# GpSimd kept to transfers in the block loop, and the pass over all tokens moved behind block 20

## The reference

```
s = attention(xn)          # 4 heads; per token and head a layernorm of 32 numbers, times gamma = 1 + ln_w
g = silu(moe(xn))          # each token goes to 1 of 8 experts:
                           #   y = (a * sigmoid(gate)) @ w2[e] + b2[e],  [a, gate] = xn @ w1[e] + b1[e]
out = x + s * g            # elementwise, per token
```

## Time and profile before

| | |
|---|---|
| median of 3 runs | 222.67 us (221.75 to 223.59) |
| the profiled execution's own time | 222.88 us |
| its span, first to last instruction | 221.0 us |
| TensorE busy | 197.2 us, 89% |
| VectorE busy | 162.3 us, 73% |
| ScalarE busy | 148.2 us, 67% |
| GpSimd busy | 127.6 us, 58% |
| mean granted TensorE clock | 0.972 of full speed |

### The profile page before, as it was taken

How to read it: one execution, slowest core, us unless ns; L and a number is a source line. 1 busy time by engine, 2 the same in 40 slices (tenths; PEclk the granted TensorE clock), 3 DMA queues, 4 the chain that set the end, 5 groups by cost and what they waited for, 6 DMA issues and landing times.

```text
span 221.0 us, 5891 instructions
## 1 busy us (share of the span) xinstructions
PE 197.2 (89%) x1790; PEld 164.7 (75%) x1790; DVE 162.3 (73%) x428; ACT 148.2 (67%) x318; POOL 127.6 (58%) x154
## 2 busy tenths in 40 slices
PE   7998998899999999999999999899999998998000
PEld 6887855355555555799999998799999997997000
DVE  5999588869688777558879989986444699987400
ACT  2388858899888798678877777467777776673000
POOL 5575960556577772003333448787677598477740
PEclk9999999999999999999999999999999999999855
DMA  5999999971499612210870667265432975511100
GB/s 165 304 391 415 390 203 208 209 186 40 147 331 353 219 62 88 82 36 27 243 246 18 187 183 207 87 189 152 121 113 74 293 269 164 158 34 47 48 0 0
DMA packets 35103, 36.96 MB, mean 167 GB/s; under 512 B 4219, under 2 KB 29828, under 8 KB 35073
## 3 DMA queue, kind: packets, MB, share of 16 engines
q1 hardware_dynamic: 29762, 26.71, 37.3%
q0 software_dynamic: 4144, 9.79, 17.9%
q10 hardware_dynamic: 1168, 0.10, 0.4%
HBM read 21.95 MB, written 15.63 MB: 170 GB/s over the span
## 4 chain that ended last, share of the span: by engine, by line
PE 54%; DVE 17%; POOL 12%; issue 7%; DMA 4%; DVEq 1%; ACT 1%; POOLq 1%; ACTq 0%
PE bank L1293 14%; PE head_bank L1293 14%; PE bank L1302 13%; POOL xs_sorted L494 9%; DVE stats L799 3%; PE bank L1263 2%; PE head_bank L1251 2%; POOL out_x L539 2%; PE head_bank L1221 2%; PE bank L1180 2%; DMA x_sb<-in_L_attn_x 1%; DVE dm L1065 1%; PE bank L1241 1%; PE head_bank L1149 1%; DVE ffn L1082 1%
## 5 line engine op out<-in xcount | busy, mean ns | idle before, releaser
L518 POOL DMA_INDIRECT y_tokens<-ffn,idx x24 | 25.6, 1067 | 40.7 <-DVE ffn L1082 34.8
L676 ACT ACTIVATE wc<-w_sb 128x1024 f32 (+1 forms) x39 | 37.8, 970 | 15.2 <-issue 15.2
L494 POOL DMA_INDIRECT xs_sorted<-xn,pos x32 | 31.4, 982 | 21.9 <-DVE pos L936 9.3
L1302 PE MATMUL bank<-w_sb,dm 128*128 x312 | 41.7, 277 | 2.5 <-DVE dm L1065 2.5
L1302 PEld LDWEIGHTS bank<-w_sb,dm 128*128 128x128 f32 x312 | 38.0, 192 | 3.4 <-issue 3.3
L1293 PE MATMUL bank<-xsT,wc 128*128 128x128 f32 x320 | 39.1, 275 | 0.0
L1293 PEld LDWEIGHTS bank<-xsT,wc 128*128 128x128 f32 x320 | 37.3, 192 | 0.2 <-issue 0.2
L964 DVE TENSOR_TENSOR cm<-dm,head_bank 128x1024 f32<-128x1024 f32 (+1 forms) x32 | 29.1, 950 | 11.1 <-PE head_bank L1251 10.0
L1293 PE MATMUL head_bank<-xsT,wc 128*128 128x128 f32 x304 | 37.0, 275 | 0.0
L1293 PEld LDWEIGHTS head_bank<-xsT,wc 128*128 128x128 f32 x304 | 35.5, 192 | 0.0
L654 ACT ACTIVATE dm<-bank 128x512 f32<-128x512 f32 x48 | 26.9, 596 | 3.8 <-PE bank L1241 3.5
(11 more groups left out here) (189 smaller groups left out, 351.1 us busy)
## 6 DMA issues: line engine op xcount, KB each, us to landing
x_sb<-in_L_attn_x SPq DMA_DIRECT2D x16, 256.0 KB, 4.8
w_sb<-in_L_ffn_w SPq DMA_DIRECT2D x8, 512.0 KB, 8.5
w_sb<-negated_rows POOLq DMA_DIRECT2D x8, 508.0 KB
xs_sb<-xs_sorted SPq DMA_DIRECT2D x13, 192.0 KB, 2.6
xs_sorted<-b_sb SPq DMA_DIRECT2D x1, 2048.0 KB, 10.8
y_tokens<-zeros SPq DMA_DIRECT2D x1, 2048.0 KB
s_and_x<-x_sb SPq DMA_DIRECT2D x16, 128.0 KB
s_and_x<-xn SPq DMA_DIRECT2D x16, 128.0 KB
```

Source lines behind the costliest of these rows:

```text
L494: pool.indirect_dma_start(xs_dram, bass.IndirectOffsetOnAxis(ap=pos[:, t:t + 1], axis=0), xn[:, t, :], None).then_inc(s_scat, 16)
L518: pool.indirect_dma_start(y_dram, bass.IndirectOffsetOnAxis(ap=idx[:, j:j + 1], axis=0), ys_sb[:, j // CH % 2, j % CH, :], None, bounds_ch ...
L676: act.activation(wc[:, j % 3, h0:H2], w1_sb[:, bass.ds(e, 1), h0:H2], ACT.Copy).then_inc(s_wc, 1)
L1302: last = pe.matmul(bank[6 + j % 2][:, 0:D], uT[:, j % 2, c, :], w2_sb[:, bass.ds(e * (HC * D) + c * D, D)], start=(c == 0), stop=(c == HC ...
```

## The change

The change does six things.

- The factor gamma leaves GpSimd. It becomes 8 more steps of the normalisation on VectorE (4 tiles each), so there are 43 steps. STEPS_AT gives two steps to each of the iterations 12 to 19, where before it did so for 12 to 15.
- All 8 sums with x are on VectorE; GpSimd had 5 of them.
- LATE is 18 where it was 15, so 21 blocks (0 to 20) are scattered to `y_tokens`, and 18 take the late way.
- The pass is placed earlier: its products in iterations 25 to 28 (before 28 to 31), its sums in 27 to 31 (before on GpSimd and in 32), the joins two by two from iteration 32 to 40.
- SyncE stores all quarters of s behind the load of the rows of blocks 27 to 29 (c = 9), each when its two steps of gamma are done. Gathers 0 and 1 stand behind scatters 18 and 19, all others behind scatter 20.
- GpSimd has a `drain` in four places: before the first scatter, before scatters 6 and 12, and before the wait for `s_out`. The drains show in no row of the orders below.

The gathered rows and the late blocks' rows find place in `u_all`, in `right` (no longer used then) and in what is left of `cm`.

```diff
-    NSTEPS = 35
-    SMALL = 27
+    NSTEPS = 43
+    SMALL = 35
-    STEPS_AT = {2: 1, 3: 1, 4: 2, 5: 1, 6: 2, 7: 1, 8: 5, 9: 5, 10: 5, 11: 4, 12: 2, 13: 2, 14: 2, 15: 2}
-    GAMMA_AT = {11: 0, 12: 1, 14: 2, 15: 3}
-    LATE = 15
+    STEPS_AT = {2: 1, 3: 1, 4: 2, 5: 1, 6: 2, 7: 1, 8: 5, 9: 5, 10: 5, 11: 4}
+    STEPS_AT.update({j: 2 for j in range(12, 20)})
+    LATE = 18
-    PRODUCTS_AT = {28: (0, 1), 29: (2, 3), 30: (4, 5), 31: (6, 7)}
-    ADDS_AT = {32: (5, 6, 7)}
-    POOL_ADDS = (0, 1, 2, 3, 4)
-    JOINS_AT = {33: (0, 1), 34: (2, 3), 35: (4, 5), 36: (6, 7), 37: (8, 9), 38: (10,), 39: (11, 12), 40: (13, 14)}
+    PRODUCTS_AT = {25: (0,), 26: (1, 2), 27: (3, 4), 28: (5, 6, 7)}
+    ADDS_AT = {27: (0,), 29: (1, 2, 3), 30: (4, 5, 6), 31: (7,)}
+    JOINS_AT = {32 + i: (2 * i, 2 * i + 1) for i in range(9)}
-    TOKENS_AT.update({17: (6, 7), 18: (8,), 20: (9,), 22: (10,), 25: (11,), 28: (12,)})
-    GATHERS_AT = {18: (0,), 19: (1,), 20: (2,), 21: (3,), 22: (4,), 23: (5, 6, 7)}
-    ROWS_AT = {8: (0,), 9: (1, 2, 3)}
+    TOKENS_AT.update({17: (6, 7), 18: (8,), 20: (9,), 23: (10,), 26: (11,), 28: (12,)})
+    GATHERS_AT = {18: (0,), 19: (1,)}
+    ROWS_AT = {9: (0, 1, 2, 3)}
...
             def s_rows(g):
-                sp.wait_ge(s_gm, g + 1)
+                sp.wait_ge(s_norm, SMALL + 2 * (g + 1))
...
             for g in range(NPC):
-                if g in POOL_ADDS:
-                    sp.wait_ge(s_finp, POOL_ADDS.index(g) + 1)
-                else:
-                    sp.wait_ge(s_finv, g + 1 - len([i for i in POOL_ADDS if i < g]))
+                sp.wait_ge(s_finv, g + 1)
...
+            pool.drain()
             pool.wait_ge(s_yz, 16)
             for j in range(JL):
+                if j in (6, 12):
+                    pool.drain()
                 pool.wait_ge(s_ye, j + 1)
...
-                if j in GAMMA_AT:
-                    scaled(GAMMA_AT[j])
...
-            gather(8)
-            add_x(0)
-            add_x(1)
-            gather(9)
-            add_x(2)
-            add_x(3)
-            gather(10)
-            add_x(4)
-            for i in range(11, LATE):
+            for i in range(2, LATE):
                 gather(i)
+            pool.drain()
             pool.wait_ge(s_out, 16 * NPC)
...
+                dve.wait_ge(s_gamma, 2)
+                for ts in pieces:
+                    yield dve.tensor_tensor(sq[:, ts, :, :], sq[:, ts, :, :],
+                                            gamma[:, :].rearrange("p (h d) -> p h d", h=NH).unsqueeze(1).to_broadcast([P, 4, NH, DH]),
+                                            ALU.mult)
```

More of the change, by code:

```diff
@@ L109, in mlstm_moe_block @@
         u_flat = u_all[:, :, :, :].rearrange("p t h c -> p (t h c)")
-        gx = u_flat[:, 0:LATE * 2 * D].rearrange("p (i c) -> p i c", c=2 * D)
+        n_u = T * NH * DA // (2 * D)
         wc = sb("wc", [P, 3, H2])
@@ L195, in mlstm_moe_block @@
         ssum, den, rden, coef, nveps, na, nb_, ny, ny2 = [cflat[:, n * T * NH:(n + 1) * T * NH] for n in range(9)]
-        lz = cflat[:, 9 * T * NH:9 * T * NH + LATE * D].rearrange("p (i d) -> p i d", d=D)
+        c_free = 9 * T * NH
+        r_flat = right[:, :, :, :].rearrange("p h j s -> p (h j s)").bitcast(F32)
+        gx = [u_flat[:, i * 2 * D:(i + 1) * 2 * D] if i < n_u else cflat[:, c_free + (i - n_u) * 2 * D:c_free + (i - n_u + 1) * 2 * D]
+              for i in range(LATE)]
+        c_free += (LATE - n_u) * 2 * D
+        n_r = NH * NBS * S // 2 // D
+        lz = [r_flat[:, i * D:(i + 1) * D] if i < n_r else cflat[:, c_free + (i - n_r) * D:c_free + (i - n_r + 1) * D]
+              for i in range(LATE)]
         ys_sb = ffn[:, 0:2 * CH * D].rearrange("p (i n d) -> p i n d", i=2, n=CH)
@@ L323, in mlstm_moe_block @@
         s_yz = sem("s_yz")
-        s_gm = sem("s_gm")
         s_sx = sem("s_sx")
@@ L328, in mlstm_moe_block @@
         s_finv = sem("s_finv")
-        s_finp = sem("s_finp")
         s_fin = sem("s_fin")
@@ L498, in gather @@
                 pool.wait_ge(s_idx, (JL + i) // CH + 1)
-                pool.indirect_dma_start(gx[:, i, :], None, sx_dram, bass.IndirectOffsetOnAxis(ap=idx[:, JL + i:JL + i + 1], axis=0),
+                pool.indirect_dma_start(gx[i], None, sx_dram, bass.IndirectOffsetOnAxis(ap=idx[:, JL + i:JL + i + 1], axis=0),
                     bounds_check=NTOK - 1, oob_is_err=False).then_inc(s_gx[i], 16)
[L502 to L512, removed]
+            pool.drain()
             pool.wait_ge(s_yz, 16)
             for j in range(JL):
+                if j in (6, 12):
+                    pool.drain()
                 pool.wait_ge(s_ye, j + 1)
@@ L539, in _ @@
                 pool.indirect_dma_start(out_rows, bass.IndirectOffsetOnAxis(ap=idx[:, JL + i:JL + i + 1], axis=0),
-                    lz[:, i, :], None, bounds_check=NTOK - 1, oob_is_err=False).then_inc(s_fin, 16)
+                    lz[i], None, bounds_check=NTOK - 1, oob_is_err=False).then_inc(s_fin, 16)
         @block.scalar
@@ L1043, in piece_product @@
                 dve.wait_ge(s_yg[g], 16)
-                dve.wait_ge(s_gm, len(GROUPS))
+                dve.wait_ge(s_norm, NSTEPS)
                 dve.tensor_tensor(yg[:, ts, :], yg[:, ts, :], xn[:, ts, :], ALU.mult).then_inc(s_prod, 1)
@@ L1055, in join @@
                 dve.wait_ge(s_ye, JL + i + 1)
-                link(dve.tensor_tensor(lz[:, i, :], lz[:, i, :], gx[:, i, 0:D], ALU.mult))
-                dve.tensor_tensor(lz[:, i, :], lz[:, i, :], gx[:, i, D:2 * D], ALU.add).then_inc(s_late, 1)
+                link(dve.tensor_tensor(lz[i], lz[i], gx[i][:, 0:D], ALU.mult))
+                dve.tensor_tensor(lz[i], lz[i], gx[i][:, D:2 * D], ALU.add).then_inc(s_late, 1)
             def product(j):
@@ L1080, in silu @@
                     dve.wait_ge(s_yst[c % NX], 16 * CH * (c // NX + 1))
-                gated = ys_sb[:, (j // CH) % 2, j % CH, :] if j < JL else lz[:, j - JL, :]
+                gated = ys_sb[:, (j // CH) % 2, j % CH, :] if j < JL else lz[j - JL]
                 dve.tensor_tensor(gated, sy[:, j % 2, :], yb[:, j % 2, :], ALU.mult).then_inc(s_ye, 1)
```

## The result

The change takes 213.91 us (median of 4 runs, 213.37 to 215.5) where the kernel before takes 223.12 (4 runs): a ratio of 0.961, interval 0.954 to 0.968. It was run twice more (e9, e17), with 0.962 (0.958 to 0.967) and 0.959 (0.951 to 0.967). A ratio leaves out executions over 1.5% slower than the fastest of their kernel; a median holds them all. I had forecast 218.2, in a range down to 216.7: the right way, 4.3 us too little. The profiled execution took 213.37 us, its span is 211.5, so 1.9 us lie around the span as before.

A forecast was written before the change was run, and what follows sets the result against it. GpSimd's output scatters were taken to bound the end, TensorE the loop before. Start at 185.3 plus 22.2 put the last scatter at 207.5 against 212.02, -4.5 us: 218.2 against the median, range 216.7 to 221.4.

The forecast's parts named there:

- What bounds the kernel now: Whole span: GpSimd's output scatters bind the last 19 us, TensorE the loop before; the 9.0 us after the last scatter's start stay.
- Both bounds for them: Cost of the added drains: between nothing and a scatter's longest landing, 5.3 us; charged as nothing.
- That the drains lie in idle time: GpSimd: first drain in 15.7 us idle, two in waits for VectorE, the last ending at worst at 184.8, under the wait.
- Gamma: Iterations 16 to 19: steps on VectorE cost nothing, TensorE's loss of 1.92 us goes, last step ends at 147.6.
- Stores of s and scatter 20: SyncE and GpSimd: gather 0 begins at 152.8, scatter 20 at 156.8; the pass's loads start at 160.8, 9.1 us earlier.
- The pass: VectorE, iterations 25 to 31: 0.1 us lateness in all, last sum ends at 181.1, output scatters may begin at 185.3.
- One sign of being wrong: VectorE: the forecast would be wrong if iterations 27 to 30 exceed 2.9 us.
- another of the signs: Wrong if the gap from the last sum to the first output scatter is not 4.2 us.
- The last scatters: GpSimd's end: 18 scatters, 17 gaps of 1.306 us, 22.2 in all; the last starts at 207.5 against 212.02.
- GpSimd didn't starve: Rival, 0.15: gathers slowed beside VectorE's two-input operations end at 186.9 to 190.1; time 219.8 to 223.0 us.
- VectorE wasn't the bound: Rival, 0.13: added gammas and sums, 8.6 us, make iterations 27 to 30 take 3.1 us each; time 219.5 us.
- The slower rival: Chance 0.06: the pass comes before its data, VectorE's wait for piece 0 stops TensorE too; 7.6 us late, 225.8 us.

The follow-up runs named there:

- e9: The change itself, unaltered, run again beside the kernel before: 214.15 us, ratio 0.962.
- e17: The change itself, run again on the same chip as the change without its drains: 213.7 us, ratio 0.959.
- e2: The change without its four drains, against the kernel before, on a chip with stops: 247.06 us, ratio 1.011.
- e5: The change without its four drains once more, against the kernel before, on a chip with stops: 249.35 us, ratio 1.021.
- e15: The change without its four drains again, against the kernel before, on a chip with stops: 248.54 us, ratio 1.013.
- e18: The change without its four drains, on the same chip as a run of the change itself: 220.43 us, ratio 0.989 to the kernel before.
- e6: The kernel before with only gamma moved to VectorE, no drains added, on a chip with stops: 243.4 us, ratio 0.989.
- e7: The kernel before with only GpSimd's five sums moved to VectorE, no drains added, on a chip with stops: 248.81 us, ratio 1.014.
- e8: The change with its sums one iteration earlier and joins from iteration 31, on a chip with stops: 240.69 us, ratio 0.985 to the kernel before.
- e11: The change with its sums one iteration earlier and a fifth drain ahead of gather 0: 217.51 us, ratio 0.979 to the kernel before.
- e16: The change with sums one iteration earlier and its four drains, repeated on a chip with stops: 241.91 us, ratio 0.986 to the kernel before.
- e1: The kernel before with only the change's four drains added, on a chip with stops: 241.09 us, ratio 0.982.
- e10: The change with 15 late blocks instead of 18, its pass and joins three iterations later: 217.65 us, ratio 0.978 to the kernel before.
- e13: The kernel before with only the four drains added, repeated on a chip with stops: 241.61 us, ratio 0.979.
- e14: The kernel before with the four drains and gamma on VectorE, on a chip with stops: 238.66 us, ratio 0.972.
- e12: The change with a fifth drain between the 9th and 10th scatter into the output: 217.56 us, ratio 0.979 to the kernel before.

## Why the prediction was wrong

- **The step that failed** is in "What bounds the kernel now": "From the start of the last scatter to the span's end it is 9.0 us, which the change leaves", and with it the drains: "I take nothing". I took the 9.0 us for a constant of every execution, without asking for the row that fills it. It is the sequencer's DRAIN, and it grows with the open transfers. I had bounded the added drains by what they could hold up, and never by what they could take from the end. Both bounds for them lay at or above nothing. (The worst end that I gave the last of them, 184.8, was too early as well: it ended at 185.2.)
- How large, from the tails: 97 open: 8.0 us (e2, e5, e15, e18); 94: 7.7 to 7.8 (before, e6, e7); 57: 4.7; 45: 3.8; 18: 1.9 (the change, e8, e9, e11, e16, e17); 15: 1.8 (e1, e10, e13, e14); 9: 1.5. From 45 to 97 that is 4.2 / 52 = 0.08 us for each transfer; at 18 and below it is the landing of the last transfer, 1.1 us behind its issue, and 0.4 to 0.7 more. Of the drains inside the change, the first (40 open) ends 3.4 us behind the last issue, on this line; the last (27 open) 3.7 us behind the last gather, above it, because a gather lands later: this one 3.8 us after its start, at 184.1, and the drain ends 1.1 behind that, as in e9, e10 and e12. Why a drain costs something for each transfer that has long landed, no run shows. 97 are the 8 accumulating transfers of w1, 32 scatters into the sorted rows, 21 into `y_tokens`, 18 gathers and 18 scatters into the output. The change ends with 18 open.
- **That the drains lie in idle time** was right for the change, and it is no property of the drains: the last one ends at 185.2 under a wait that lasts until 186.3. It was close: where a drain holds the first scatter, that comes 0.9 us behind the drain's end (e1, e11, e12), and here it came 1.1 behind, 1.0 in e9. In the kernel before, the same drain held the scatters by 2.2 us (e1), and with a fifth one behind scatter 18 the change took 3.4 us more (e11).
- **Gamma**: right. The beat held through iterations 12 to 19, the first loss of 1.92 went, and the last step of gamma ended at 148.3 (147.6 worked out).
- **Stores of s and scatter 20**: 1.3 us later than worked out (gather 0 at 154.02 for 152.8, scatter 20 at 158.07 for 156.8), and it cost nothing, since the last load of sorted rows set the start of the loads, as I had it.
- **The pass**: pieces 3 and 4 came late, VectorE waited 1.0 us for them, and the last sum ended at 182.78 in place of 181.1. I had checked pieces 0 and 1 and no others. (16 gathers now run beside the loads; that they slow them is argued, not shown.) One sign of being wrong came true here: iteration 27, with that wait, took 4.2 us and not 2.9 at most (VectorE's products of iterations 27 and 28 start at 168.40 and 172.62). From the last sum to the first scatter it took 3.5 us, not 4.2, another of the signs. The start was 186.3 for 185.3.
- **The last scatters**: 17 gaps in 22.08 us, 1.299 each for 1.306. Last start 208.38 for 207.5. By the schedule alone the time would have been 218.2 + 0.9 = 219.1; e18, the change without drains, took 220.43 on its own chip.
- **The rivals**: GpSimd didn't starve in the change: the gathers took 1.00 to 1.43 us, and their pitch from 159.39 to 180.27 was 1.39 for the 1.34 taken; begun 1.3 late, they ended at 181.5 for 179.5. But it can: gathers of 1.9 to 2.5 us stand in e12, e15 and e18, each beside three operations of the pass, and in e12 they delayed the end. That none stood in the traces of the change is partly luck. VectorE wasn't the bound: iterations 29 and 30, with three pieces each, took 2.8 us. The slower rival wasn't there in the change; e11 shows its wait for piece 0.

## What to carry to other kernels

When a sum is made against a span, name the row that fills each part of it, the end behind the last busy instruction too: the page leaves out the sequencers, the query by line shows them. In a kernel in which GpSimd issues many transfers, look at where its last DRAIN ends; here each open transfer cost 0.08 us at the end, and a drain paid it for nothing where it ended 1 us or more ahead of what GpSimd had to do next, while a run with one on the path lost 2 to 3.4 us. Where a drain stands behind transfers that land late, as the gathers here, it ends no earlier than they do. A chain that ends in a count of issues after a start gains from an earlier start, less the issues that this adds: 3 blocks earlier bought 9.7 us and cost 4.2 (e9 against e10).

## What was not expected of the hardware

In this kernel a DRAIN at the end of GpSimd's program takes 0.08 us for each transfer issued since the last drain, from 45 to 97 of them, even though all had landed up to 6.9 us before its end. With 6 to 9 open a drain still ends 1.4 to 3.4 us behind the last issue; where the landing is on record it ends 0.2 to 0.5 us behind that. On TensorE's weight queue, ScalarE and VectorE the same instruction at the end took 0.81, 0.34 and 0.33 us.

A gather issued beside three operations of VectorE on two inputs took up to 2.5 us (e12, e15, e18) and beside the same three in the change 1.0 to 1.3; what decides it no run shows.

On some chips the same kernel took 245 and not 223 us, with stops of 2 to 10 us at several engines that no row of the core explains; ratios between variants weren't the same there (the change without drains: 1.011 to 1.021 against 0.989).
